# Reading the norm roots back for two head pairs in one load instead of one load per head pair

## The reference, cut to what matters

```python
def l2norm(t):
    return t / jnp.maximum(jnp.linalg.norm(t, axis=-1, keepdims=True), 1e-12)

def attn_layer(x, Wqkv, qs, ksc, Wo):
    q, k, v = jnp.split(x @ Wqkv, 3, -1)
    q, k, v = (sh(q), sh(k), sh(v))
    q = l2norm(q) * qs
    k = l2norm(k) * ksc
    q = q * cos * scale + rotate_half(q) * sin * scale
    k = k * cos / scale + rotate_half(k) * sin / scale
    out = local_attention(q, k, v)
    return out.transpose(0, 2, 1, 3).reshape(b, n, INNER) @ Wo
```

## Time and profile before

| | |
|---|---|
| median of 3 runs | 3383.88 us (3381.18 to 3386.66) |
| the profiled execution | 3385.34 us |
| its span, first to last instruction | 3383.5 us |
| TensorE (PE) busy | 3179.4 us, 94% |
| ScalarE (ACT) / VectorE (DVE) / GpSimd (POOL) busy | 2557.1 / 2411.4 / 2216.2 us |
| mean granted TensorE clock | 0.983 of full speed |
| RB loads | 768 transfers of 128 KB, 3.0 us to landing in the median |

### The profile page before, as it was taken

One profiled execution on the slowest core, in us unless ns is written; L12 is line 12 of the kernel. 1 busy time (PEld: TensorE's weight loads), 2 busy tenths in 40 slices (PEclk: granted clock), 3 DMA queues, 4 the chain that ended last, 5 costly groups with the idle time before them and its releaser, 6 DMA issues.

```text
span 3383.5 us, 125778 instructions
## 1 busy us (share of the span) xinstructions
PE 3179.4 (94%) x52744; PEld 1944.9 (57%) x52744; DVE 2411.4 (71%) x2940; ACT 2557.1 (76%) x5866; POOL 2216.2 (65%) x2135
## 2 busy tenths in 40 slices
PE   7999996899999999999999999999999999999996
PEld 3444442566666666666666666666666666656653
DVE  3656654677777777777777777777777777777773
ACT  5666663687877878887778887878787888788884
POOL 0000003877788777788777887778887778877771
PEclk9999997899999999999999999999999999999998
DMA  3232322444445444554444544444544454544441
GB/s 112 76 81 72 80 71 72 161 157 147 156 154 165 151 152 152 162 162 161 149 152 155 167 157 158 148 155 157 167 153 158 150 162 158 160 149 157 149 141 40
DMA packets 290260, 472.26 MB, mean 140 GB/s; under 512 B 90398, under 2 KB 128540, under 8 KB 289564
## 3 DMA queue, kind: packets, MB, share of 16 engines
q1 hardware_dynamic: 263376, 447.69, 41.6%
q10 hardware_dynamic: 26316, 16.52, 1.7%
HBM read 124.21 MB, written 7.34 MB: 39 GB/s over the span
## 4 chain that ended last, share of the span: by engine, by line
PE 56%; DVE 10%; ACT 8%; SPq 8%; POOL 7%; issue 5%; DMA 5%; POOLq 0%; ACTq 0%; DVEq 0%
PE PS L542 56%; DMA RB<-root_scratch 4%; POOL K L1314 2%; DVE TPB L938 2%; DVE H L990 2%; SPq L528 2%; ACT SC L1227 2%; SPq L499 2%; POOL Q L1332 2%; ACT SX L1203 1%; ACT H L1263 1%; SPq L531 1%; SPq L507 1%; SPq L517 1%; ACT AOT L1240 1%
## 5 line engine op out<-in xcount | busy, mean ns | idle before, releaser
L938 DVE SCALAR_TENSOR_TENSOR TPB<-PS,VEC,C 128x1024 f32<-128x1024 f32 x768 | 970.8, 1275 | 413.4 <-ACT SX L1203 400.6
L1227 ACT ACTIVATE SC<-PS,BQ,RQ 128x64 f32<-128x64 f32 x3072 | 964.0, 431 | 2.8 <-POOL BQ L1350 2.7
L1203 ACT ACTIVATE SX<-PS 128x512 f32<-128x512 f32 x768 | 461.8, 614 | 282.8 <-PE PS L542 282.0
L1314 POOL TENSOR_TENSOR K<-K,RB 128x512 f32<-128x512 f32 x384 | 492.8, 1283 | 153.9 <-DMA RB<-root_scratch 148.3
L1332 POOL TENSOR_TENSOR K<-TPB,TR 128x512 f32<-128x512 f32 x384 | 494.6, 1288 | 0.0
L1332 POOL TENSOR_TENSOR Q<-TPB,TR 128x512 f32<-128x512 f32 x384 | 493.1, 1284 | 0.0
L542 PE MATMUL PS<-LXH,LH 128*128 128x512 f32 x768 | 403.8, 526 | 49.6 <-DVE TPB L938 34.0
L1358 POOL TENSOR_TENSOR SC<-SC,RC 128x1024 f32<-128x1024 f32 x192 | 366.3, 1908 | 29.4 <-DVE RC L961 29.1
L542 PE MATMUL PS<-AOT,LO 128*128 128x512 f32 x768 | 370.0, 605 | 0.0
L542 PEld LDWEIGHTS PS<-PP,VV 64*64 64x64 f32 x12288 | 271.8, 133 | 154.6 <-issue 152.6
L542 PE MATMUL PS<-PP,VV 64*64 64x96 f32 (+1 forms) x12288 | 340.5, 246 | 1.9 <-issue 0.8
(11 more groups left out here) (169 smaller groups left out, 5672.9 us busy)
## 6 DMA issues: line engine op xcount, KB each, us to landing
TR<-TPB SPq DMA_DIRECT2D x768, 256.0 KB, 3.0
RB<-root_scratch SPq DMA_DIRECT2D x768, 128.0 KB, 3.0
PP<-PX SPq DMA_DIRECT2D x1344, 64.0 KB, 2.0
WS<-in_wqkv ACTq DMA_DIRECT2D x72, 128.0 KB, 2.7
PP<-PX SPq DMA_DIRECT2D x192, 48.0 KB, 2.0
QA<-TH SPq DMA_DIRECT2D x128, 64.0 KB, 2.1
QA<-TL SPq DMA_DIRECT2D x128, 64.0 KB, 2.1
KA<-TH SPq DMA_DIRECT2D x128, 64.0 KB, 2.1
```

The source lines that it names most:

```text
L938: e.scalar_tensor_tensor(TPB[:, n % 3:4 + n % 2:3 + n % 2 - n % 3, w, :], g, VEC[:, l, 9 + w:10 + w], C[:, at:at + 1024].rearrange("p (o c ...
L1203: e.activation(SX[i % 3][:, :], bk("PJ", key)[:, :], ACT.Square).then_inc(sem["pj_act"], 1)
L1227: p = e.activation(SC[m % 2][:, g, :, :].rearrange("p x k -> p (x k)"), bank[s][:, at:at + 64], ACT.Exp, bias=BQ[m % 2][:, g:g + 1], scale ...
L1314: e.tensor_tensor(dst, dst, RB[n % 2][:, :], ALU.mult).then_inc(sem["pr_pool"], 1)
```

## The change

The root rows of two head pairs (2m and 2m+1) are loaded together. The rows for one head position of these two pairs lie next to each other in `root_scratch`, so one piece of 4 KB holds both. RB becomes a stage of every second n, due at 2m-2.851, with two transfers of 64 pieces of 4 KB (256 KB each) in place of four transfers of 128 KB. Its target is one tile RB of [128, 2, 512], of the same total size as the two tiles before. The load of pair number p = m waits until PR(2p-1) is done (before: PR(n-2)), since there is one buffer for both. PR(2p) and PR(2p+1) both wait for that load. The semaphores rb_in0 and rb_in1 are now told apart by the parity of p, and RW waits by that count.

```diff
         lay(n + P["TS"], o.put, "TS", n)
-        lay(n + P["RB"], o.put, "RB", n)
         lay(n + P["PR"], o.put, "PR", n)
...
-            for st in ("S1", "MX", "BQ", "SU", "NP", "TT", "PX", "PVn"):
+            for st in ("RB", "S1", "MX", "BQ", "SU", "NP", "TT", "PX", "PVn"):
                 lay(n + P[st], o.put, st, m)
...
-        RB = [sb(f"RB{i}", [128, L]) for i in range(2)]
+        RB = sb("RB", [128, 2, L])
...
                 elif st == "RW":
                     q, = key
                     if q > 1:
-                        for n in (4 * q - 6, 4 * q - 5):
-                            on.wait_ge(f"rb_in{n % 2}", 32 * (n // 2) + 32)
+                        for i in range(2):
+                            on.wait_ge(f"rb_in{i}", 32 * q - 32)
...
                 elif st == "RB":
-                    n, = key
-                    q = n // 4
-                    if n > 1:
-                        on.wait_ge("pr_pool", n - 1)
+                    p, = key
+                    q = p // 2
+                    if p:
+                        on.wait_ge("pr_pool", 2 * p)
                     on.wait_ge(f"rr_in{q % 2}", 64 * (q // 2) + 64)
-                    at = 8 + 4 * (n % 4 // 2) + n % 2
                     for s in range(2):
-                        r = rootd[q % 2, at + 2 * s:at + 2 * s + 1, :]
-                        e.dma_start(RB[n % 2][64 * s:64 * s + 64, :], r.broadcast_to([64, L])).then_inc(sem[f"rb_in{n % 2}"], 16)
+                        at = 8 + 4 * (p % 2) + 2 * s
+                        r = rootd[q % 2:q % 2 + 1, at:at + 2, :].rearrange("o e k -> o (e k)")
+                        e.dma_start(RB[64 * s:64 * s + 64, :, :].rearrange("p e k -> p (e k)"),
+                                    r.broadcast_to([64, 2 * L])).then_inc(sem[f"rb_in{p % 2}"], 16)
...
                     on.wait_ge("ad_pool", 2 * n + 2)
-                    on.wait_ge(f"rb_in{n % 2}", 32 * (n // 2) + 32)
-                    e.tensor_tensor(dst, dst, RB[n % 2][:, :], ALU.mult).then_inc(sem["pr_pool"], 1)
+                    p = n // 2
+                    on.wait_ge(f"rb_in{p % 2}", 32 * (p // 2) + 32)
+                    e.tensor_tensor(dst, dst, RB[:, n % 2, :], ALU.mult).then_inc(sem["pr_pool"], 1)
```

## The result

| | before | after |
|---|---|---|
| median | 3386.56 us (6 runs, 3381.18 to 3392.36) | 3419.61 us (6 runs, 3403.72 to 3432.36) |
| ratio | | 1.0094 (95% interval 1.0064 to 1.0123) |
| profiled execution, span | 3385.34 us, 3383.5 us | 3418.67 us, 3416.9 us |
| RB transfers, median to landing | 768, 3.0 us | 384, 4.1 us |

The kernel is slower by 0.94%, some 32 us. The forecast was 3377 us with a range of 3362 to 3395, and the measured median lies above it. Two of the prediction's own signs of being wrong came: a landing of 4 us and more, and over 40 us of waiting for K on TensorE.

The account below looks back on a forecast made before the run. TensorE, busy 2590 of 2700 us in the layers, was taken as the bound; 0.40 us landing minus 0.69 us relief at 29 waits, capped, gave -7 us on 3385.34, 3378; forecast 3377 us, range 3362 to 3395.

Parts of the forecast that it names:

- the size of the landing: At RB's merged loads: 256 KB in place of 128 KB lands 0.4 us later, range 0.2 to 1.3 us.
- the pace of the issue: At RB's loads behind TS: 128 KB per 0.62 us of issue sets their rate, so only a 0.32 us tail is added.
- The rival with 1.3 us: At RB(4q)'s landing: one DRAM row can't be read faster, 1.3 us in 47 units, +23 us, 3407 us; chance 0.22.
- The two figures that fitted so well: At RB's loads behind TS: 211 GB/s from the issue pace and some 200 GB/s seen, taken as support for the issue pace.
- The relief: On SP ahead of PX and RW: without RB(4q-1), RB(4q) is issued 0.69 us sooner in the mean at 29 units.
- the prediction's sum: TensorE's waits for K, unit by unit: relief against longer landing, -7 us in all.
- the forecast's case: Whole kernel: relief outweighs the longer landing, -14 to -1 us, chance 0.50.
- nobody pays: At RB(4q+2), which now waits for PR(4q+1): the TS behind it is issued 1.9 us after that RB is through, costing nothing.
- the second groups' slack behind RB(4q): At second groups: S1 starts over 1 us after PR(4q+1), so 0.4 us of later PR(4q) costs nothing.
- PP's readers: At the matmuls reading PP, loaded by PX: they wait for nothing today, so an earlier PX gives nothing.
- second groups make no wait: At second groups of a unit: TensorE has no wait for K there; the waits lie at first groups of 29 units.

Follow-up runs that it names:

- half-size kernel: Changed kernel with each load bringing only the even pair's row (128 KB), odd pairs scaled by the even pair's roots: 3368.19 us, ratio 0.9944 to the kernel before.
- e14: Kernel before, nothing merged, only RB(4q+3) moved to right behind RB(4q+2): 3383.61 us, ratio 0.9977.

## Why the prediction was wrong, point by point

- **The step that failed is the size of the landing.** The text took 0.4 us and held with the pace of the issue, as "the larger pieces fill the gaps and only the tail of the last one is added"; the landing grew by 1.1 us. The rival with 1.3 us had the right place and nearly the right price (and 3407 us where 3420 were measured), but the reason it gave, one DRAM row, was wrong too: different rows land in 4.2 us. The target partitions were the cause, shown by 4.1 to 3.3 us and 39 us of time; what it is in 64 neighbouring partitions, no run shows. The two figures that fitted so well, 211 GB/s of issue and 200 GB/s of throughput, could not be told apart in the earlier trace rows; the comparison with TS's 400 GB/s left out that TS goes to every other partition and RB to 64 neighbours.
- **The relief was right in size.** RW starts 0.11 us after the roots at first groups in place of 0.89, so 0.78 us sooner in the median, close to the 0.69 us of the sum. With the landing at 3.3 us, 0.3 us more, the prediction's sum lies between -11 us (0.2) and -7 us (0.4), and the kernel on every other partition is 7 us faster (ratio 0.9980). The half-size kernel gained 19 to 21 us, more than the -14 us at the good end of the forecast's case, but there TS lands faster too, so it is no clean measure of the relief.
- **The sensitivity of the whole time was too small.** The same sum gives +9 us for 0.9 us and +23 us for 1.3, so about +16 us for 1.1; measured 32 us. For what the sum priced, TensorE's waits for K, it was right: they grew by 17.4 us, 14 of them at first groups. Missing is what it priced at nothing. The waits under "issue" grew by 12 us. And the prediction found that PR(4q+2) starts long after its load and that "nobody pays". Alone the gate costs nothing (3389 us), but the merged load at that place costs 16 to 18 us against before, and some 24 us against the same order with single loads (e14). In the changed kernel 14 of 51 passages of the chain through RB end at PR(4q+2), and 10 of these run on over the roots into RW; before it was 7 of 32, and 2. That this path is how the time is lost is read from the chain; with the load merged at this place alone the time was lost without a longer wait for K, under "issue", and who is waited for there stays open.
- **The 4 KB pieces** were worth nothing either way (3418 with 2 KB against 3419 us).
- **Right**: GpSimd's multiply keeps its 1.28 us; odd PRs don't wait; SP's issues ahead of PX and RW were on the path, since moving them without saving them gives 6 us; the second groups' slack behind RB(4q) (of the changed kernel's waits for K, read singly, 27 with 39 us lie behind RB(4q) of first groups and 3 with 2 us behind that of second ones; two more, of 1.8 and 4.7 us, lie behind RB(4q+2)); PP's readers don't wait for its transfers by name. But their wait under "issue" grew by 7 us, of all matmuls by 12 us, which I had not counted. Not quite right was that second groups make no wait in the kernel before: two of the 32 waits lie there, with 2.9 us.
- **Left open**: the changed kernel with two full tiles (no gate, large loads) was not tried; so how much of the 16 us at the second place comes from the one buffer together with the slow load is not measured. Nor is it known whom PP's readers wait for, nor why the first load of the layers has the same throughput on either set of partitions and a different landing.

## What to carry to other kernels

Look at which partitions a transfer writes before merging it: here the same 256 KB took 4.1 us to 64 neighbouring partitions and 3.3 to every other one, while for loads of 128 KB the same choice was worth 0.1 us (3.0 and 2.9). Here the layout asks for the neighbouring ones, so this was a reason not to merge. A merged load makes its first reader wait for the bytes of the second. If what helps is the queue's order, move the issue and leave the transfers as they are (6 us faster here). And price a slower landing at every reader, with the gate ahead of it, not only where TensorE waits today.

## What the runs showed of the hardware

Pieces of 2 or 4 KB at the same transfer size, and one DRAM row or 64, made no difference that can be measured in the landing (4.1, 4.1 and 4.2 us). With 64 rows the queue's share of the DMA engines was a little higher, at 128 KB 43.3% in place of 41.6%. Merging two 128 KB loads saved the issue time in full (1.20 us for two loads of 256 KB, as for two of 128 KB), so what it costs is in the landing and in what shares the engines: TS landed in 3.4 in place of 3.0 us.
